# A macaron layer on one core: the second half's gathers moved behind the first half's returns, shared units split, all stages re-placed

## Chip, cores, metric

The kernel runs on one core of a Trainium2 chip. The metric is the device time of one execution in microseconds (us). TensorE is called PE, VectorE DVE, ScalarE ACT, GpSimd POOL and SyncE SP, as the profile does.

## What is computed

`x` has 4 batches of 512 tokens of width 128 (2048 tokens). The layer is a "macaron": half a feed-forward layer, attention, half a feed-forward layer, each on a layer-normalised input, each added to `x`:

```python
x = x + 0.5 * _L0_ffn_ref(_layernorm(x), ...)
x = x + _L0_attn_ref(_layernorm(x), ...)
x = x + 0.5 * _L0_ffn_ref(_layernorm(x), ...)

# _L0_ffn_ref, 8 experts, the best 2 of them per token, and one shared expert for all
probs = softmax(x_flat @ gate_w.T)
top_w, sel = jax.lax.top_k(probs, 2)
top_w = top_w / sum(top_w)
y = gelu(x_flat @ W1[e] + b1[e]) @ W2[e] + b2[e]      # weighted by top_w for the chosen e
out = sum(y * combine) + gelu(x_flat @ sW1 + sb1) @ sW2 + sb2
```

The attention has 8 query heads on 2 key heads and looks back 32 tokens within a batch, with a sink in the softmax.

## The kernel before

**Blocks and units.** Each of the two feed-forward layers is done in two halves of 1024 tokens (two batches). That gives four blocks, numbered 0 to 3: blocks 0 and 1 are the first layer, 2 and 3 the second. A block has 23 routed units (a tile of up to 128 tokens for one expert; here R0 to R3, name `("R", block, 0, RT)` in `ORDER`) and 8 shared units (4 for each of its two batches; S0 to S3). A unit has a first product (`first_product`, into the PSUM tile `z`), a gelu on ACT, and two steps later (`LAG`) a second product (`second_product`, into `y`).

**Steps.** `ORDER` numbers all 124 units; the number is the unit's step. Each engine runs a loop over the steps, and what else it does stands in a table: `PE_AT`, `ACT_AT`, `DVE_AT`, `POOL_AT` and `SP_AT` give each stage a step (behind the point its place in the step). Within a step the tables set the order of the instructions; the time comes from semaphores alone. Before: S0 has the steps 0 to 7, R0 8 to 30, R1 31 to 53, S1 54 to 61, R2 62 to 84, S2 85 to 92, R3 93 to 115, S3 116 to 123.

**The way of a routed block.** SP stores the normalised rows to `xr` (stage `rows`, `store_rows`). The router runs: PE turns the tokens (`tr`), makes logits, DVE picks the experts (`pick`, `gap`), PE counts positions (`pos`), DVE places them (`place`), PE tells the slots (`idx`), DVE makes the lists of experts (`tiles`, tile `te`) and of rows (`final`, `know_rows`). Then POOL fetches each unit's rows with an indirect DMA (`gather`, tile `xg`); PE turns two units' rows at a time (`xtr`, `turn_rows`), ACT evicts them (`xevict`, tile `xgt`), SP copies the expert's first weights into `w1_tile` (`copy_weights`; the profile writes `w_tile`). The result goes to `ysb` on ACT and back to DRAM by an indirect DMA of POOL (`give_back`, `yd`), one unit per step and three steps after its first product. When a block's last returns have landed, SP loads them (`load_y`, tile `yc`, which the profile calls `stage`), and DVE adds them to `x` (`comb`).

**What follows a block.** After block 0 DVE's combine gives `x` for the attention of batches 0 and 1 (`att_stats`, `att_pow` on POOL, `att_xn` on ACT, `att_tr` on PE, and on to `proj` and `xadd`), which runs among the units of R1; then block 2's router needs those. After block 1 the same goes for batches 2 and 3, among R2. Blocks 2 and 3 end in `comb` and a store.

**Lead of gathers and copies.** `ahead(r, by)` gives the step at which unit r's gather stands on POOL (8 routed units ahead) and its weight copy on SP (4 ahead), and no sooner than `KNOWN[block]`. A ring of 8 slots holds the rows (`xg`), one of 6 the weights.

Of the kernel before, what the change touches and what calls it, by code (L numbers as in the profile page):

```python
# [64 lines left out]
def routed_no(ph, i):  # L65
# [5 lines left out]
    ('pos', 0): 1.01, ('idx', 0): 6.51, ('xtr', 0, 0): 7.54, ('xtr', 0, 1): 8.51, ('xtr', 0, 2): 9.51,  # L71
    ('tr', 1, 0): 9.53, ('tr', 1, 1): 9.535, ('tr', 1, 2): 10.51, ('tr', 1, 3): 10.515, ('logits', 1): 11.51,
    ('turn_w',): 12.51, ('xtr', 0, 3): 13.51, ('xtr', 0, 4): 13.53, ('xtr', 0, 5): 13.54, ('pos', 1): 14.51,
    ('xtr', 0, 6): 18.01, ('idx', 1): 19.01, ('xtr', 0, 7): 20.01, ('xtr', 0, 8): 20.02, ('xtr', 0, 9): 25.51,
    ('xtr', 0, 10): 26.51, ('xtr', 0, 11): 28.51, ('xtr', 1, 0): 28.52, ('xtr', 1, 1): 32.51, ('xtr', 1, 2): 34.51,
# [1401 lines left out]
```

How the kernel before makes its waits and increments, by code:

```python
        def moved(eng, k):  # L340
            eng.wait_ge(m_done[k % MB], k // MB + 1)
# [5 lines left out]
        def result_out(eng, u):  # L348
            eng.wait_ge(y_used[Y_USE[u] % 2], Y_USE[u] // 2 + 1)
# [1 line left out]
        def landed(eng, r):  # L352
            eng.wait_ge(returned[r % YR], 16 * (r // YR + 1))
# [29 lines left out]
            def store_biases():  # L384
                sp.wait_ge(b_hi_done, 1)
                sp.dma_start(bd[0], b_hi[:, :]).then_inc(b_stored, 16)
                sp.wait_ge(b_split, 1)
                sp.dma_start(bd[1], b_lo[:, :]).then_inc(b_stored, 16)
# [1 line left out]
            def load_biases():  # L391
                sp.wait_ge(b_stored, 32)
                sp.dma_start(wb2[:, :, :], bd).then_inc(b_ready, 16)
# [16 lines left out]
            def store_rows(ph):  # L411
                for j in range(2):
                    sp.wait_ge(pre_lo_done, 2 * ph + j + 1)
                    rows = slice(j * TT * P, (j + 1) * TT * P)
                    sp.dma_start(xr[ph][rows].rearrange("(t p) r -> p t r", p=P), xs[ph % 2][:, TT * j:TT * (j + 1)])\
                        .then_inc(rows_stored[ph], 16)
# [1 line left out]
            def copy_weights(r):  # L418
                ph, _, i, _ = UNITS[ROUTED[r]]
                if i == 0:
                    sp.wait_ge(te_ready, ph + 1)
                if r == 0:
                    sp.wait_ge(w1_split, E)
                    sp.wait_ge(b1_ready, 1)
                if r >= WR:
                    sp.wait_ge(z_ready, ROUTED[r - WR] + 1)
                    sp.wait_ge(gelu_done, ROUTED[r - WR] + 1)
```

## Time and profile before

| | us |
|---|---|
| median of 3 runs (lowest, highest) | 375.26 (374.29, 377.11) |
| the profiled execution, its own time | 374.08 |
| span of the profiled execution, first to last instruction | 372.3 |
| PE busy in the span | 314.2 (84%) |
| ACT busy | 240.8 (65%) |
| POOL busy | 203.9 (55%) |
| DVE busy | 170.5 (46%) |

The median is 1.18 us above the profiled execution, and that one is 1.8 us longer than its span. A busy PE is not PE at its peak: ends of matmuls are modelled, and the engine also counts as busy at the half clock. All times in the rows below are from the span's start.

### The profile page before, as it was taken

To read this page: it belongs to the slowest core of one execution; us is meant where nothing else is said; L and a number is where in the kernel's file an instruction comes from. 1 tells how busy PE (TensorE), PEld (TensorE's weight loads), DVE (VectorE), ACT (ScalarE), POOL (GpSimd) and SP (SyncE) were. 2 spreads that over 40 slices of the span, in tenths; PEclk is the share of its full clock that TensorE was granted. 3 is DMA by queue.
4 is the path that set the end of the run, shared out by engine and by line. 5 is a ranking of instruction groups with operands and counts; after the bars stand their busy time and mean duration, and the time that the engine had idled before them with its cause. 6 is when DMAs were issued, how large, how long until landed. Compare 5 with 4: busy or idle time off the path is not lost.

```text
span 372.3 us, 10763 instructions
## 1 busy us (share of the span) xinstructions
PE 314.2 (84%) x3591; PEld 269.3 (72%) x3599; DVE 170.5 (46%) x623; ACT 240.8 (65%) x666; POOL 203.9 (55%) x220
## 2 busy tenths in 40 slices
PE   0692999999736998999895789999999699979991
PEld 0372988989636867899775588899888488868881
DVE  6997248400026479464782658826457330000005
ACT  4971577778624968959531787995974268847640
POOL 5206677777774875124417775745442577776500
PEclk9996799999976899999996999999999989989998
DMA  7793755555263244101136233324223745553131
GB/s 233 233 240 94 258 175 169 153 195 184 79 197 128 96 161 106 66 37 57 61 128 223 97 102 125 103 85 136 89 65 107 261 139 193 194 141 104 37 121 56
DMA packets 39222, 50.51 MB, mean 136 GB/s; under 512 B 5803, under 2 KB 23296, under 8 KB 39170
## 3 DMA queue, kind: packets, MB, share of 16 engines
...
## 4 chain that ended last, share of the span: by engine, by line
PE 52%; POOL 13%; issue 11%; DVE 11%; ACT 6%; DMA 6%; SPq 1%; DVEq 0%; ACTq 0%
PE y L619 16%; POOL xg L498 7%; PE z L583 5%; POOL yd L506 5%; PE y L634 4%; PE z L585 4%; PE z L584 4%; PE m L801 3%; PE y L622 3%; DVE x L1212 2%; DMA xg<-xr,from_row 2%; PE m L680 2%; PE m L654 2%; ACT h L877 2%; PE m L789 2%
## 5 line engine op out<-in xcount | busy, mean ns | idle before, releaser
L877 ACT ACTIVATE h<-z,w_tile 128x128 f32<-128x128 f32 x368 | 105.2, 373 | 40.0 <-PE z L585 37.6
L506 POOL DMA_INDIRECT yd<-ysb,to_row x92 | 91.7, 997 | 58.0 <-ACT ysb L890 38.6
L498 POOL DMA_INDIRECT xg<-xr,from_row x92 | 91.4, 993 | 58.6 <-issue 40.8
L619 PE MATMUL y<-w,h 128*128 x736 | 105.2, 288 | 0.0
L619 PEld LDWEIGHTS y<-w,h 128*128 128x128 f32 x736 | 93.0, 197 | 1.4
L583 PE MATMUL z<-xgt,w_tile 128*128 128x128 f16 x368 | 71.0, 229 | 12.1 <-ACT xgt L934 5.6
L584 PE MATMUL z<-xgt,w_tile 128*128 128x128 f16 x368 | 70.6, 227 | 0.0
L585 PE MATMUL z<-xgt,w_tile 128*128 128x128 f16 x368 | 70.6, 227 | 0.0
L583 PEld LDWEIGHTS z<-xgt,w_tile 128*128 128x128 f16 x368 | 37.2, 101 | 19.5 <-issue 8.6
L934 ACT ACTIVATE xgt<-m 128x512 f16<-128x512 f16 (+1 forms) x48 | 27.1, 590 | 25.0 <-PE m L680 24.8
L1112 DVE SCALAR_TENSOR_TENSOR x<-y,x 128x512 f32<-128x512 f32 x8 | 5.5, 690 | 79.7 <-PE y L639 79.7
L634 PEld LDWEIGHTS y<-w,h 128*128 128x128 f32 x256 | 35.9, 207 | 3.4
L1212 DVE SCALAR_TENSOR_TENSOR x<-stage,s_gate,x 128x128 f32<-128x128 f32 x64 | 19.1, 362 | 40.8 <-DMA stage<-yd 39.7
L585 PEld LDWEIGHTS z<-xgt,w_tile 128*128 128x128 f16 x368 | 37.6, 102 | 0.0
L584 PEld LDWEIGHTS z<-xgt,w_tile 128*128 128x128 f16 x368 | 37.4, 102 | 0.1
L634 PE MATMUL y<-w,h 128*128 128x128 f32 x256 | 36.9, 292 | 0.0
L882 ACT ACTIVATE h<-z,sb 128x512 f32<-128x512 f32 x32 | 21.9, 687 | 21.8 <-PE z L656 21.8
L680 PE MATMUL m<-ident,xg 128*128 128x128 f16 x184 | 19.2, 229 | 19.6 <-DMA xg<-xr,from_row 19.5
L890 ACT ACTIVATE ysb<-y 128x128 f32<-128x128 f32 x92 | 26.3, 286 | 12.6 <-PE y L622 11.6
L487 POOL TENSOR_TENSOR rstd<-ve,half 128x4 f32<-128x4 f32 x12 | 12.8, 1070 | 31.6 <-DVE ve L1081 31.5
L680 PEld LDWEIGHTS m<-ident,xg 128*128 128x128 f16 x184 | 11.9, 101 | 23.9 <-DMA xg<-xr,from_row 11.8
L914 ACT ACTIVATE xn<-x,nmr,rstd 128x128 f32<-128x128 f32 x48 | 19.7, 482 | 10.3 <-DVE nmr L1086 5.9
...
## 6 DMA issues: line engine op xcount, KB each, us to landing
...
xg<-xr,from_row POOLq DMA_INDIRECT x92, 2.7
yd<-ysb,to_row POOLq DMA_INDIRECT x92, 2.6
...
```

The source lines that it names most:

```text
L498: pool.indirect_dma_start(out=xg[:, r % XR, :], out_offset=None, in_=xr[ph], in_offset=bass.IndirectOffsetOnAxis(ap=from_row[:, ph, i:i + ...
L506: pool.indirect_dma_start(out=yd[ph], out_offset=bass.IndirectOffsetOnAxis(ap=to_row[:, ph, i:i + 1], axis=0), in_=ysb[:, r % YR, :], in_o ...
L583: pe.matmul(part, w[:, c, :], hi, start=(c == 0), stop=False, skip_group_check=True)
L584: pe.matmul(part, w[:, c, :], lo, start=False, stop=False, skip_group_check=True)
L585: op = pe.matmul(part, w[:, FC + c, :], hi, start=False, stop=True, skip_group_check=True)
L619: pe.matmul(to, h32[:, u % HB, c * P:(c + 1) * P], w2[:, bass.ds(e, 1), c, :].rearrange("p a d -> p (a d)"), start=(c == 0), stop=False, s ...
L634: op = pe.matmul(to[:, t * D:(t + 1) * D], h32[:, u % HB, t * P:(t + 1) * P], w2[:, SHARED, c, :], start=(c == 0 and t == 0), stop=False, ...
L680: op = pe.transpose(bank16(k)[:, at:at + P], xg[:, r % XR, part * D:(part + 1) * D], ident16[:, :])
L877: op = act.activation(h32[:, u % HB, cols], z[:, u % 2, cols], ACT.Gelu, bias=bias[:, c:c + 1], scale=1 / WS)
L890: act.activation(ysb[:, r % YR, :], y[:, Y_USE[u] % 2, 0:D], ACT.Copy).then_inc(y_used[Y_USE[u] % 2], 1)
L934: act.activation(xgt[:, (ph * PAIRS + q) % XT, 0:n].rearrange("p t k d -> p (t k d)"), bank16(k)[:, 0:2 * n * P], ACT.Copy)\
L1212: op = dve.scalar_tensor_tensor(to, yc[:, t, k, :], s_gate[:, ph, k, t:t + 1], to, ALU.mult, ALU.add)
```

## The change

It does four things. First, S1 and S3 are split: the first batch's four shared units stand ahead of the block's routed units, the other four behind them. After: S0 0 to 7, R0 8 to 30, first half of S1 31 to 34, R1 35 to 57, second half of S1 58 to 61, R2 62 to 84, S2 85 to 92, first half of S3 93 to 96, R3 97 to 119, second half of S3 120 to 123. Second, `KNOWN` is split in two lists, one for gathers and one for weight copies, and its second entry goes from 19 to 33, so that no row of block 1 is fetched before all of block 0's returns have been issued. Third, every stage gets a new place in all five tables. Fourth, SP's `rows` of block 1 goes from step 10 to 7. No computation is added or left out, and no tile changes its size.

```diff
-ORDER = [("S", 0, 0, 1), ("R", 0, 0, RT), ("R", 1, 0, RT), ("S", 1, 0, 1), ("R", 2, 0, RT), ("S", 2, 0, 1), 
-         ("R", 3, 0, RT), ("S", 3, 0, 1), ("none", 8)]
+ORDER = [("S", 0, 0, 1), ("R", 0, 0, RT), ("S", 1, 0), ("R", 1, 0, RT), ("S", 1, 1), ("R", 2, 0, RT), 
+         ("S", 2, 0, 1), ("S", 3, 0), ("R", 3, 0, RT), ("S", 3, 1), ("none", 8)]
...
-    ('gap', 3): 84.44, ('place', 3): 85.15, ('gates', 3): 89.37, ('tiles', 3): 89.45, ('final', 3): 90.14,
-    ('comb', 2, 0): 91.67, ('comb', 2, 1): 95.54, ('comb', 3, 0): 131, ('comb', 3, 1): 131.2,}
+    ('gates', 3): 90.73, ('tiles', 3): 90.85, ('comb', 2, 0): 91.62, ('final', 3): 92.98, ('comb', 2, 1): 95.67,
+    ('comb', 3, 0): 131, ('comb', 3, 1): 131.2,}
...
-    ('attention',): 0, ('rows', 1): 10, ('load_y', 0): 34, ('rows', 2): 52, ('load_y', 1): 57, ('rows', 3): 81,
-    ('load_y', 2): 88, ('store', 0): 95, ('store', 1): 99, ('load_y', 3): 119, ('store', 2): 131, ('store', 3): 131.5,}
+    ('attention',): 0, ('rows', 1): 7, ('load_y', 0): 34, ('rows', 2): 53, ('load_y', 1): 61, ('rows', 3): 83,
+    ('load_y', 2): 88, ('store', 0): 95, ('store', 1): 99, ('load_y', 3): 123, ('store', 2): 131, ('store', 3): 131.5,}
...
-KNOWN = [7, 19, 60, 90]
+ROWS_FROM, WEIGHTS_FROM = [7, 33, 61, 93], [7, 33, 61, 93]
...
-def ahead(r, by):
-
-    return max(STEP[ROUTED[max(r - by, 0)]], KNOWN[UNITS[ROUTED[r]].ph])
+def ahead(r, by, no_sooner):
+
+    return max(STEP[ROUTED[max(r - by, 0)]], no_sooner[UNITS[ROUTED[r]].ph])
...
-                    if ahead(r, WEIGHTS_AHEAD) == n:
+                    if ahead(r, WEIGHTS_AHEAD, WEIGHTS_FROM) == n:
                         copy_weights(r)
...
-                    if ahead(r, ROWS_AHEAD) == n:
+                    if ahead(r, ROWS_AHEAD, ROWS_FROM) == n:
                         gather(r)
```

Line numbers of the changed kernel are two higher than those of the kernel before.

**POOL, at the end of block 0.** `yd0` and `yd1` are the returns of blocks 0 and 1, `xr0` and `xr1` the stored rows that a gather reads. In the kernel before, from the last gather of block 0 on:

```order
L498 DMA xg<-xr0,from_row 128x256
L506 DMA yd0<-ysb,to_row 4992x128
L498 DMA xg<-xr1,from_row 128x256
L506 DMA yd0<-ysb,to_row 4992x128
L498 DMA xg<-xr1,from_row 128x256
```

and so on by turns for all 11 returns that are left, and then five turns with `yd1` before `L487 TENSOR_TENSOR rstd` (the powers of the attention's norm) is all through. In the changed kernel:

```order
L500 DMA xg<-xr0,from_row 128x256
L508 DMA yd0<-ysb,to_row 4992x128 x11
L500 DMA xg<-xr1,from_row 128x256 x11
L489 TENSOR_TENSOR rstd<-ve,half 128x4 x2
L508 DMA yd1<-ysb,to_row 4992x128
L500 DMA xg<-xr1,from_row 128x256
```

The 11 last returns of block 0 now stand in a row, then 11 gathers of block 1, then both powers, and only then the turns of returns and gathers of block 1.

**SP, ahead of the first routed unit.** `xr1<-xs1` is the store of block 1's rows, `w1_tile<-w1` the copy of a unit's weights, for which SP first loads the unit's expert from `te`. In the kernel before:

```order
L409 DMA sink<-in_L0_attn_sink_bias_dram 128x1
L429 TENSOR_LOAD te
L429 ISA x2
L430 ISA
L430 DMA w1_tile<-w1 128x516
```

and after six such copies `L415 DMA xr1<-xs1 128x4x256 x2`. In the changed kernel:

```order
L411 DMA sink<-in_L0_attn_sink_bias_dram 128x1
L417 DMA xr1<-xs1 128x4x256 x2
L431 TENSOR_LOAD te
L431 ISA x2
L432 ISA
L432 DMA w1_tile<-w1 128x516
```

The two stores have moved from behind the sixth copy to ahead of the first.

**DVE, at the same place.** `w<-stage,w` (`split_lo`) makes the low part of one expert's weights, `padded`, `from_row` and `to_row` are `final`, `xs<-xn,xs` the low part of block 1's rows that SP's stores wait for. In the kernel before:

```order
L1184 TENSOR_SCALAR te<-count 128x23 [waits router0]
L1232 SCALAR_TENSOR_TENSOR w<-stage,w 128x512 [waits w1_hi_done]
L1190 SCALAR_TENSOR_TENSOR padded<-m,pad 128x23 [waits m_ready]
L1192 CAST from_row<-m 128x23 [waits router0]
L1193 TENSOR_TENSOR to_row<-m,padded 128x23
L1232 SCALAR_TENSOR_TENSOR w<-stage,w 128x512 [waits m_done3,w1_hi_done]
L1232 SCALAR_TENSOR_TENSOR w<-stage,w 128x512 [waits w1_hi_done] x5
L1095 TENSOR_TENSOR xs<-xn,xs 128x4x128 [waits pre_hi_done] x2
```

In the changed kernel:

```order
L1186 TENSOR_SCALAR te<-count 128x23 [waits router0]
L1192 SCALAR_TENSOR_TENSOR padded<-m,pad 128x23 [waits m_ready]
L1194 CAST from_row<-m 128x23 [waits router0]
L1195 TENSOR_TENSOR to_row<-m,padded 128x23
L1234 SCALAR_TENSOR_TENSOR w<-stage,w 128x512 [waits m_done3,w1_hi_done]
L1234 SCALAR_TENSOR_TENSOR w<-stage,w 128x512 [waits w1_hi_done] x6
L1097 TENSOR_TENSOR xs<-xn,xs 128x4x128 [waits pre_hi_done] x2
```

Seven of the eight low parts stand behind `final` now, where six did.

## Rows read from the trace of the kernel before

**Rows 1.** PE's waits: what waited for what, us in total, times, longest.
```profile
PE m L680 <- DMA xg<-xr,from_row: 19.5, 11, 3.8
```
**Rows 2.** Chain that ended last, in order of time: start us, us, what.
```profile
105.77 4.00 DMA stage<-yd
...
119.17 0.63 PE m L735 x4
...
345.97 0.95 PE y L619 x8
347.85 0.95 PE y L619 x8
...
354.85 0.89 PE y L634 x8
356.39 0.89 PE y L634 x8
```
**Rows 3.** PE's timeline: start us, us, instruction, count, [idle before, what ended it].
```profile
20.30 1.05 PE L634 MATMUL y<-w,h 128*128 128x128 f32 x8
...
36.45 0.27 PE L583 MATMUL z<-xgt,w_tile 128*128 128x128 f16 x1 [1.69 <-DMA w_tile<-w]
...
37.68 2.02 PE L634 MATMUL y<-w,h 128*128 128x128 f32 x8
...
93.11 0.22 PE L622 MATMUL y<-wb,ones 2*128 x1
...
194.71 0.50 PE L634 MATMUL y<-w,h 128*128 128x128 f32 x3
...
199.87 0.29 PE L583 MATMUL z<-xgt,w_tile 128*128 128x128 f16 x1 [0.69 <-ACT xgt L934]
...
278.18 0.38 PE L654 MATMUL z<-xt,sw 128*128 128x512 f16 x1
```
**Rows 4.** SP's timeline of DMA issues: the first weight copies, block 1's rows, block 3's load.
```profile
33.52 6.75 SPq L430 DMA_DIRECT2D w_tile<-w  x6
40.31 1.22 SPq L415 DMA_DIRECT2D xr<-xs  x2
...
355.60 0.93 SPq L441 DMA_DIRECT2D stage<-yd  x2
```
**Rows 5.** DVE's timeline: low parts, block 3's lists and combine, the last combine.
```profile
28.84 3.70 DVE L1232 SCALAR_TENSOR_TENSOR w<-stage,w 128x512 f16<-128x512 f32 x6
32.46 1.34 DVE L1095 TENSOR_TENSOR xs<-xn,xs 128x512 f16<-128x512 f32 x2
...
289.60 0.17 DVE L1190 SCALAR_TENSOR_TENSOR padded<-m,pad 128x23 f32<-128x23 f32 x1
...
290.33 2.33 DVE L1212 SCALAR_TENSOR_TENSOR x<-stage,s_gate,x 128x128 f32<-128x128 f32 x8 [0.25 <-DVE to_row L1193]
...
365.06 4.53 DVE L1212 SCALAR_TENSOR_TENSOR x<-stage,s_gate,x 128x128 f32<-128x128 f32 x16
```
**Rows 6.** POOL's timeline: returns (yd), gathers (xg) and a power (rstd).
```profile
103.43 0.98 POOL L506 DMA_INDIRECT yd<-ysb,to_row  x1 [0.30 <-issue]
...
115.85 1.04 POOL L487 TENSOR_TENSOR rstd<-ve,half 128x4 f32<-128x4 f32 x1 [5.02 <-DVE ve L1081]
...
194.61 0.99 POOL L498 DMA_INDIRECT xg<-xr,from_row  x1 [8.10 <-issue]
...
290.90 1.00 POOL L498 DMA_INDIRECT xg<-xr,from_row  x1 [7.45 <-issue]
...
332.00 0.97 POOL L498 DMA_INDIRECT xg<-xr,from_row  x1 [0.30 <-issue]
...
353.20 0.97 POOL L506 DMA_INDIRECT yd<-ysb,to_row  x1 [0.84 <-ACT ysb L890]
```
**Rows 7.** DMA issues of the page: KB each, median us from issue to landing.
```profile
xg<-xr,from_row POOLq DMA_INDIRECT x92, 2.7
```
**Rows 8.** Span and mean granted clock of the core.
```profile
core 0: 372.3 us, clock 0.945
```

More of the change, by code:

```diff
@@ L70 @@
 PE_AT = {
[L71 to L75, printed above, removed]
@@ L89 @@
-    ('xtr', 2, 9): 79.51, ('tr', 3, 0): 79.52, ('tr', 3, 1): 79.525, ('xtr', 2, 10): 79.53, ('xtr', 2, 11): 79.54,
-    ('tr', 3, 2): 81.51, ('tr', 3, 3): 81.515, ('logits', 3): 82.51, ('pos', 3): 84.51, ('idx', 3): 89.51,
-    ('xtr', 3, 0): 92.51, ('xtr', 3, 1): 93.51, ('xtr', 3, 2): 96.51, ('xtr', 3, 3): 96.52, ('xtr', 3, 4): 96.53,
-    ('xtr', 3, 5): 101.01, ('xtr', 3, 6): 102.01, ('xtr', 3, 7): 104.51, ('xtr', 3, 8): 105.51, ('xtr', 3, 9): 107.01,
-    ('xtr', 3, 10): 110.51, ('xtr', 3, 11): 110.52,}
@@ new lines @@
+    ('pos', 0): 2.51, ('idx', 0): 7.01, ('xtr', 0, 0): 7.51, ('tr', 1, 0): 7.52, ('tr', 1, 1): 7.525,
+    ('tr', 1, 2): 7.53, ('tr', 1, 3): 7.535, ('xtr', 0, 1): 7.54, ('xtr', 0, 2): 9.51, ('xtr', 0, 3): 13.01,
+    ('xtr', 0, 4): 13.02, ('xtr', 0, 5): 13.03, ('logits', 1): 13.51, ('xtr', 0, 6): 15.01, ('xtr', 0, 7): 17.51,
+    ('xtr', 0, 8): 22.01, ('xtr', 0, 9): 23.51, ('pos', 1): 24.51, ('xtr', 0, 10): 25.01, ('xtr', 0, 11): 26.51,
+    ('idx', 1): 32.51, ('turn_w',): 32.52, ('xtr', 1, 0): 34.51, ('xtr', 1, 1): 36.51, ('xtr', 1, 2): 36.52,
@@ new lines @@
+    ('xtr', 1, 3): 37.51, ('xtr', 1, 4): 38.01, ('att_tr', 0): 39.51, ('att_tr', 1): 40.51, ('qk', 0): 40.52,
+    ('v', 0): 40.53, ('qk', 1): 41.01, ('scores', 0, 0): 43.01, ('scores', 0, 1): 43.02, ('xtr', 1, 5): 44.51,
+    ('v', 1): 44.52, ('xtr', 1, 6): 46.51, ('scores', 1, 0): 46.52, ('scores', 1, 1): 46.53, ('pt', 0, 0): 47.51,
+    ('pv', 0, 0): 48.51, ('pt', 0, 1): 48.52, ('xtr', 1, 7): 48.53, ('xtr', 1, 8): 48.54, ('pt', 1, 0): 48.55,
+    ('pv', 0, 1): 48.56, ('pt', 1, 1): 48.57, ('pv', 1, 0): 48.58, ('proj', 0): 48.59, ('pv', 1, 1): 48.6,
@@ new lines @@
+    ('xtr', 1, 9): 48.61, ('xtr', 1, 10): 48.62, ('proj', 1): 50.01, ('tr', 2, 0): 52.01, ('tr', 2, 1): 52.015,
+    ('xtr', 1, 11): 53.51, ('tr', 2, 2): 53.52, ('tr', 2, 3): 53.525, ('logits', 2): 55.01, ('pos', 2): 57.01,
+    ('idx', 2): 61.51, ('xtr', 2, 0): 61.52, ('xtr', 2, 1): 62.51, ('xtr', 2, 2): 64.51, ('att_tr', 2): 64.52,
+    ('qk', 2): 66.51, ('att_tr', 3): 67.51, ('xtr', 2, 3): 67.52, ('v', 2): 67.53, ('xtr', 2, 4): 67.54,
+    ('v', 3): 68.51, ('xtr', 2, 5): 68.52, ('qk', 3): 69.01, ('scores', 2, 0): 69.51, ('scores', 2, 1): 69.52,
@@ new lines @@
+    ('xtr', 2, 6): 70.51, ('xtr', 2, 7): 70.52, ('scores', 3, 0): 74.01, ('scores', 3, 1): 74.02, ('pt', 2, 0): 75.01,
[3 rows of a table added]
+    ('tr', 3, 3): 83.515, ('xtr', 2, 11): 83.53, ('logits', 3): 83.54, ('pos', 3): 85.51, ('idx', 3): 91.01,
+    ('xtr', 3, 0): 96.01, ('xtr', 3, 1): 97.51, ('xtr', 3, 2): 98.01, ('xtr', 3, 3): 99.51, ('xtr', 3, 4): 100.51,
+    ('xtr', 3, 5): 104.01, ('xtr', 3, 6): 106.01, ('xtr', 3, 7): 109.01, ('xtr', 3, 8): 110.01, ('xtr', 3, 9): 114.51,
+    ('xtr', 3, 10): 114.52, ('xtr', 3, 11): 116.01,}
@@ L138 @@
 POOL_AT = {
[L139 to L141 removed]
+    ('att_pow', 0): 38.11, ('att_pow', 1): 38.82, ('xres', 0): 41.17, ('xres', 1): 41.57, ('pow', 4): 49.48,
+    ('pow', 5): 51.87, ('att_pow', 2): 63.18, ('att_pow', 3): 66.37, ('xres', 2): 69.59, ('xres', 3): 69.78,
+    ('pow', 6): 79.04, ('pow', 7): 81.74,}
```

95 lines of the change are left out of this document (42 added, 53 removed), and 6 rows, old and new, of the table PE_AT.

## The prediction

> **What bounds the kernel now.** I read PE's waits first. The longest entry is PE waiting for gathered rows, 19.5 us in 11 waits [rows 1]. Then the chain that ended last: between a return of POOL at 103.43 and the load of block 0's results at 105.77 nothing but POOL's turns of returns and gathers leads it [rows 2, 6]. PE's timeline shows why. The last result of block 0 is finished at 93.11 + 0.22 = 93.33 [rows 3]; its return is issued at 103.43 [rows 6], ten microseconds later. A gather or a return costs POOL 1.284 us: from 290.90 to 332.00 stand 21 gathers and 11 returns, 41.10 / 32 [rows 6]. A turn of both is 2.57 us, while PE does a routed unit in 347.85 - 345.97 = 1.88 and a shared one in 356.39 - 354.85 = 1.54 [rows 2]. So where both stand on POOL, POOL sets the pace; elsewhere PE does. The attention of batches 0 and 1 hangs on the last return: combine, power at 115.85 [rows 6], PE's turn of the normalised tokens at 119.17 [rows 2].
>
> I follow five points: last return of block 0, first unit of R2 (before: 199.87), first unit of S2 (278.18) [rows 3], last return of block 3 (353.20) [rows 6], end (372.3).
>
> **Start: +3.2.** R0's first product waits for the first weight copy until 36.45 [rows 3]. That copy is issued at 33.52, right after the last low part, 28.84 + 3.70 = 32.54 [rows 4, 5]. Now one more low part (3.70 / 6 = 0.62) stands behind `final`, and I let `final` come 0.6 later, since PE tells the slots behind one more first product: low parts end at 33.8. Then SP must first store block 1's rows, which need the next two DVE instructions (1.34 [rows 5]): 35.1. The second store takes 1.22 / 2 = 0.61 [rows 4], the way to the first copy 33.52 - 32.54 = 0.98: 36.7, which is 3.2 late. Ends: 0, if the stage was covered by something I overlook, and 4.4, if the stores also hold the copy's data back by their 1.22. First product at 39.65.
>
> **R0 and its returns: -7.7.** From the first product to the last result it took 93.33 - 36.45 = 56.9. Three small pieces leave the block (slots of block 1, turned weights, one pair of turned rows); I take 1.5 for them, between 0 and one unit's 1.88. Result at 95.05, return 0.6 later (copy and issue, an allowance): 95.7 instead of 103.43. POOL keeps up: its 12 turns end as before, and the 10 returns behind gain 1.88 - 1.28 = 0.6 each on PE.
>
> **Head of R1.** The first gather of block 1 follows at 97.0. In R2 the first product came 199.87 - 194.61 = 5.26 after the first gather [rows 3, 6], so R1 starts at 102.3; PE has four shared units of S1 in front and waits for some 2 to 3 us. The combine can start 105.77 + 4.00 - 103.43 = 6.34 after the last return [rows 2, 6]: 102.0. But both powers now stand behind 11 gathers, three of which wait for turned rows: 97.0 + 11 x 1.26 = 110.9. DVE is no earlier, since the combine's second half waits behind the result of S1's first half, which PE makes in R1's second step. Power at 110.9 instead of 115.85. From there to PE's turn it was 119.17 - 115.85 = 3.32: 114.2; I take 114.5, as PE itself gets there at about 114. That is 4.7 early, of the 7.7. Ends: 7.7, if gathers and DVE wait for nothing, and 0, if they wait for each other. Block 1's first four weight copies now stand on SP just ahead of the load of block 0's results. They wait for slots that are free by then, and the shared units cover them: nothing; without the cover one costs 6.75 / 6 = 1.13 [rows 4].
>
> A rule of the Trainium skill speaks against such a row of gathers (page "SBUF — State Buffer", section "Who interferes with whom"): a DVE instruction with two SBUF inputs blocks a GpSimd instruction that reads SBUF. In the row, a gather issued beside the combine at 290.33 took 1.00 against 0.97 for one beside no such instruction [rows 5, 6]. By the row the burst loses nothing; by the rule it could lose up to the two combines beside it, 2 x 2.33 = 4.7, which is the time of the second rival.
>
> **To R2: -4.3.** After its turn at 119.17 PE worked until 194.71 + 0.50 = 195.21, 76.0 us [rows 2, 3]. What is left there now is 18 routed and 4 shared units in place of 15.7 and 8: 40.0 against 41.8, and one more pair of rows (0.2): -1.6. So PE is through at 114.5 + 74.4 = 188.9. But the slots of block 2 now come in the last step, so that no unit covers the way to R2: 0.1 + (290.90 - 289.60 = 1.3) from `final` to a gather [rows 5, 6], then 5.26: 6.7, where PE waited 199.87 - 195.21 = 4.7 before. R2 starts at 195.6. Ends for the 6.7: 5.3 (no list in the way) and 9.1 (an addition and a combine of 2.33 in it, as at R3).
>
> **R2: +1.0.** It took 278.18 - 199.87 = 78.3 [rows 3], and its work stays. The attention starts some 3 us later in it, and the router's logits stand right behind their turned tokens; I add 1.0, between 0 and one routed unit. S2 starts at 274.9, 3.3 early.
>
> **S2 to the last return: 0.0.** Before, the first gather came 290.90 - 278.18 = 12.7 after S2's first unit. Now lists of experts (1.3, as long as the way from `final` to the gather; an estimate) and a combine (2.33 + 0.25) stand ahead of `final` on DVE: 16.6. The first half of S3 covers this, so PE waits less at R3's head. But POOL's row is the same: 22nd gather 332.00 - 290.90 = 41.1 after the first, landing 2.7 or somewhat more [rows 7]: 44.3. Behind it PE has five routed units (9.4), one pair of rows, two steps with a shared unit (1.85 each) and the return (0.6): 14.1 in all. Last return 58.4 after the first gather, 62.3 before. 16.6 + 58.4 = 75.0, as before (353.20 - 278.18).
>
> **Tail: -5.5.** Before, 19.1 us followed the last return, as eight shared units stood behind. Now four do, and the way of the data is longer: load issued 355.60 - 353.20 = 2.4 later [rows 4, 6], 4.0 in flight [rows 2], combine 4.53, and 372.3 - 369.59 = 2.7 to the end [rows 5]: 13.6. PE's last products and the addition end about 1 us before the load lands. End for this term: -4, if the load takes longer.
>
> **Sum.** -3.3 + 0.0 - 5.5 = -8.8: a span of 363.5. The profiled execution was 1.78 longer than its span and 1.18 under the median: 366.5.
>
> **Rivals.**
>
> The start costs nothing (0.10): DVE's low parts end no later, or the copy isn't what R0 waits for. Against it speaks the wait of 1.69 for it [rows 3]. Then 363.3.
>
> The head of R1 eats the gain (0.22): 11 gathers, the powers behind them and the combine behind S1's result wait for each other, and the attention starts no earlier than before. For it: POOL, DVE and PE are each in order, and three gathers wait for PE. 366.5 + 4.7 = 371.2, at the edge of what can be told.
>
> The clock falls (0.11), the one that ends on the other side. The mean granted clock was 0.945 [rows 8], so (1 - 0.945) x 2 x 372.3 = 41 us at the lower of two levels, 1.2 GHz. There eight half products took 2.02 instead of 1.05 [rows 3]: 0.48 us are lost per us if PE sets the pace. R0's head was at this level after PE had waited, and now the heads of R0 and R2 wait longer and R1's anew. If the three together stay low 27 us longer, two thirds of what there was, it costs 13.0: 379.5. It decides from 26 us on; with less it only eats the gain. Against it: at the head of R3 the wait shrinks. The Trainium skill (page "TensorE: Matmul & The Clock Gate", section "HAM oscillation — how this bites in real kernels") has idle gaps bring the lower clock, at a loss of half the time spent there; the rows agree with 0.48.
>
> That the change doesn't do what it says is in the second rival: gathers behind returns are of use only if the attention starts earlier.
>
> **Chances.** Forecast 0.57, its own range 362 to 371. A measurement of this kernel can tell about 1% from no change, that is outside 371.5 to 379.0. Faster: 0.55 of the forecast, 0.10, and half of the second rival: 0.76. Same: the rest of these, 0.13. Slower: 0.11. The range for 8 in 10 reaches from 361.5 over the second rival to 374.5; the clock's case is left out.
>
> **What would show it.** Right: the first weight copy at about 36.7; POOL's last `yd` of block 0 near 95.7 and no gather of block 1 before; the first power near 111, ended by POOL's own queue; a wait of PE for gathered rows of some 6 us at R2's head; no wait at R3's head; block 3's load landing after PE's last product. Wrong: a power at 115 or later, R2's first unit at 200 or later, a clock under 0.90 at the heads' stretches taken together, or POOL's last returns behind PE by more than a unit.

## The result and the profile after

The changed kernel is a little faster: median 372.90 us (371.55 to 374.86, 12 runs), against 376.53 us (374.29 to 377.72, 12 runs) for the kernel before. The ratio is 0.9913, interval 0.9892 to 0.9933: 0.9%, where 2.3% were forecast. The direction was right, the size was not.

The profiled execution of the kernel before (374.08) lay 2.4 under the median of these 12 runs, that of the changed kernel (373.84) 0.9 over its own. So the spans (372.3 and 372.1) show almost none of the gain, and a difference of two us between the two traces is not a finding by itself. Some kernels had executions over 1.5% slower than their fastest (one of 6 in experiment 5, 3 of 12 in experiment 6, two of 6 in the first run of experiment 10, among them the one that was traced); they count in the medians, but not in the ratios.

The core's span and clock answer to [rows 8], PE's waits to [rows 1]:

```profile
core 0: 372.1 us, clock 0.943
```

```profile
PE m L682 <- DMA xg<-xr,from_row: 18.4, 11, 5.8
...
PE z L585 <- DMA w_tile<-w: 2.7, 1, 2.7
PE m L771 <- DVE v L1265: 2.4, 1, 2.4
```

The wait for gathered rows, which the edits were aimed at, went from 19.5 to 18.4. There are still 11 waits, and the longest grew from 3.8 to 5.8. Two waits are new or longer: the first weight copy, and one for `v`. The mean clock is nearly the same (0.945 before).

PE's timeline at the points followed, beside [rows 3]:

```profile
41.34 0.27 PE L585 MATMUL z<-xgt,w_tile 128*128 128x128 f16 x1 [2.72 <-DMA w_tile<-w]
...
100.78 0.27 PE L682 MATMUL m<-ident,xg 128*128 128x128 f16 x2 [0.70 <-DMA xg<-xr,from_row]
104.38 0.29 PE L682 MATMUL m<-ident,xg 128*128 128x128 f16 x2 [3.33 <-DMA xg<-xr,from_row]
105.36 0.29 PE L585 MATMUL z<-xgt,w_tile 128*128 128x128 f16 x1 [0.69 <-ACT xgt L936]
...
106.61 2.02 PE L636 MATMUL y<-w,h 128*128 128x128 f32 x8
...
119.64 0.30 PE L737 MATMUL m<-ident,xn 128*128 128x128 f32 x1 [0.52 <-ACT xn L916]
...
200.67 0.27 PE L585 MATMUL z<-xgt,w_tile 128*128 128x128 f16 x1 [0.81 <-ACT xgt L936]
...
281.29 0.61 PE L656 MATMUL z<-xt,sw 128*128 128x512 f16 x1
...
342.28 0.29 PE L682 MATMUL m<-ident,xg 128*128 128x128 f16 x2 [1.24 <-DMA xg<-xr,from_row]
...
343.86 2.02 PE L621 MATMUL y<-w,h 128*128 x8
```

Both second products of 2.02 stand behind a wait of PE and take twice what others take (1.05 in [rows 3]): they ran at the lower of the two clocks.

POOL's timeline, beside [rows 6]:

```profile
96.31 0.97 POOL L508 DMA_INDIRECT yd<-ysb,to_row  x1 [0.84 <-PE m L717]
97.66 0.98 POOL L500 DMA_INDIRECT xg<-xr,from_row  x1 [0.38 <-issue]
98.95 0.96 POOL L500 DMA_INDIRECT xg<-xr,from_row  x1 [0.30 <-issue]
...
102.70 0.97 POOL L500 DMA_INDIRECT xg<-xr,from_row  x1 [0.30 <-issue]
103.98 0.95 POOL L500 DMA_INDIRECT xg<-xr,from_row  x1 [0.30 <-issue]
...
112.55 0.94 POOL L500 DMA_INDIRECT xg<-xr,from_row  x1 [2.63 <-PE m L682]
116.39 1.04 POOL L489 TENSOR_TENSOR rstd<-ve,half 128x4 f32<-128x4 f32 x1 [2.89 <-DVE ve L1083]
...
222.19 2.50 POOL L514 TENSOR_TENSOR xres<-x,bo 128x512 f32<-128x512 f32 x2
...
297.53 1.00 POOL L500 DMA_INDIRECT xg<-xr,from_row  x1 [10.36 <-issue]
...
358.39 0.97 POOL L508 DMA_INDIRECT yd<-ysb,to_row  x1 [0.84 <-ACT ysb L892]
```

SP's DMA issues (beside [rows 4]) and DVE's timeline (beside [rows 5]):

```profile
34.95 0.97 SPq L417 DMA_DIRECT2D xr<-xs  x2
37.25 19.78 SPq L432 DMA_DIRECT2D w_tile<-w  x12
...
98.65 0.92 SPq L443 DMA_DIRECT2D stage<-yd  x2
```

```profile
29.98 4.30 DVE L1234 SCALAR_TENSOR_TENSOR w<-stage,w 128x512 f16<-128x512 f32 x7
...
102.51 2.32 DVE L1214 SCALAR_TENSOR_TENSOR x<-stage,s_gate,x 128x128 f32<-128x128 f32 x8 [4.40 <-DMA stage<-yd]
111.99 0.69 DVE L1114 SCALAR_TENSOR_TENSOR x<-y,x 128x512 f32<-128x512 f32 x1 [7.16 <-PE y L641]
112.59 2.31 DVE L1214 SCALAR_TENSOR_TENSOR x<-stage,s_gate,x 128x128 f32<-128x128 f32 x8
...
221.25 4.12 DVE L1254 TENSOR_SCALAR stage<-q_hi,head 128x512 f16<-128x512 f16 x4
```

The points side by side, us from the start of the span:

| point | before | forecast | after | after - before |
|---|---|---|---|---|
| R0's first product | 36.45 | 39.65 | 41.34 | +4.9 |
| last return of block 0 | 103.43 | 95.7 | 96.31 | -7.1 |
| first power of the attention | 115.85 | 110.9 | 116.39 | +0.5 |
| PE's turn of the normalised tokens | 119.17 | 114.5 | 119.64 | +0.5 |
| R2's first unit | 199.87 | 195.6 | 200.67 | +0.8 |
| S2's first unit | 278.18 | 274.9 | 281.29 | +3.1 |
| last return of block 3 | 353.20 | 349.9 | 358.39 | +5.2 |
| end | 372.3 | 363.5 | 372.1 | -0.2 |

The first term came true (-7.1 of -7.7 at the last return) and was gone twenty us later, at the attention's power. R2 and R3 then lost 4.4, and the tail gave 5.4 back. The experiments take these places one by one.

### The profile page after: what moved, and what is told of

Its sections match the earlier page's. It is cut to its first block, busy times and chain, and to the rows that moved or that the text cites. A ratio compares the mean times of both kernels' runs of the same rounds, so it can differ in the third digit from the quotient of the medians.

```text
span 372.1 us, 10771 instructions
## 1 busy us (share of the span) xinstructions
PE 315.5 (85%) x3599; PEld 268.9 (72%) x3599; DVE 173.6 (47%) x623; ACT 239.9 (64%) x666; POOL 202.2 (54%) x220
## 4 chain that ended last, share of the span: by engine, by line
PE 42%; POOL 16%; DVE 14%; issue 12%; DMA 9%; ACT 6%; SPq 1%; DVEq 0%; POOLq 0%; ACTq 0%
PE y L621 12%; POOL xg L500 9%; POOL yd L508 6%; DMA xg<-xr,from_row 5%; PE z L585 4%; PE m L803 3%; PE z L587 3%; PE z L586 3%; PE y L636 3%; DVE stage L1254 2%; PE y L624 2%; PE m L791 2%; ACT h L879 2%; DVE x L1214 2%; DMA x<-in_L_attn_x_dram 2%
## 5 line engine op out<-in xcount | busy, mean ns | idle before, releaser
L500 POOL DMA_INDIRECT xg<-xr,from_row x92 | 89.8, 976 | 60.4 <-issue 38.8
L621 PE MATMUL y<-w,h 128*128 x736 | 103.6, 285 | 0.0
L585 PE MATMUL z<-xgt,w_tile 128*128 128x128 f16 x368 | 70.1, 227 | 10.9 <-issue 4.3
L587 PE MATMUL z<-xgt,w_tile 128*128 128x128 f16 x368 | 69.8, 226 | 0.0
L586 PE MATMUL z<-xgt,w_tile 128*128 128x128 f16 x368 | 69.7, 226 | 0.0
L636 PE MATMUL y<-w,h 128*128 128x128 f32 x256 | 37.9, 298 | 0.0
L682 PE MATMUL m<-ident,xg 128*128 128x128 f16 x184 | 19.4, 226 | 18.5 <-DMA xg<-xr,from_row 18.4
L682 PEld LDWEIGHTS m<-ident,xg 128*128 128x128 f16 x184 | 11.7, 100 | 22.7 <-issue 12.7
L1214 DVE SCALAR_TENSOR_TENSOR x<-stage,s_gate,x 128x128 f32<-128x128 f32 x64 | 18.1, 347 | 8.4 <-DMA stage<-yd 8.0
```

The source lines that it names most:

```text
L500: pool.indirect_dma_start(out=xg[:, r % XR, :], out_offset=None, in_=xr[ph], in_offset=bass.IndirectOffsetOnAxis(ap=from_row[:, ph, i:i + ...
L585: pe.matmul(part, w[:, c, :], hi, start=(c == 0), stop=False, skip_group_check=True)
L586: pe.matmul(part, w[:, c, :], lo, start=False, stop=False, skip_group_check=True)
L587: op = pe.matmul(part, w[:, FC + c, :], hi, start=False, stop=True, skip_group_check=True)
L621: pe.matmul(to, h32[:, u % HB, c * P:(c + 1) * P], w2[:, bass.ds(e, 1), c, :].rearrange("p a d -> p (a d)"), start=(c == 0), stop=False, s ...
L636: op = pe.matmul(to[:, t * D:(t + 1) * D], h32[:, u % HB, t * P:(t + 1) * P], w2[:, SHARED, c, :], start=(c == 0 and t == 0), stop=False, ...
```

## The experiments

All start from the changed kernel unless something else is said. The diffs show table entries only. Each ratio is to runs of the kernel before on the same chip as the experiment, whose median there was between 376.1 and 377.4 us.

### 1. The stores of block 1's rows put back

```diff
-    ('rows', 1): 7
+    ('rows', 1): 10
```

> The changed kernel, with SP's store of block 1's rows put back from step 7 to step 10, behind the first weight copies. Theory (the stores hold up the first copy, and what R0 loses at its start goes through to the end): first copy issued near 34.6 instead of 37.25, first routed product near 38 instead of 41.34, last return of block 0 near 93.0 instead of 96.31, and the time 3 us under the changed kernel's, ratio to the kernel before 0.983. Rival (later waits swallow the start): last return of block 0 earlier by 3, R2's first unit where it was (200.7), ratio 0.991.

Measured: 371.48 us, ratio 0.9856 (0.9819 to 0.9893). SP's first weight copy and, in R3, POOL's first return of block 3:

```profile
35.36 6.56 SPq L432 DMA_DIRECT2D w_tile<-w  x6
```

```profile
311.12 1.01 POOL L508 DMA_INDIRECT yd<-ysb,to_row  x1 [2.75 <-ACT ysb L892]
```

The stores cost 37.25 - 35.36 = 1.9; the first product came at 39.56. R2 (198.28) and S2 (278.87) started 2.4 sooner, but the last return of block 3 only 0.5 sooner (357.86). POOL was ahead there: its first eleven gathers were through, and it waited 2.75 for the first result of R3, where the change waits 0.60. PE's wait for rows at R3's head (1.55) was followed by the lower clock, which held that first result back. So in this execution a gain at the start was waited away at R3's head. The gain came as far as S2, which is against the rival; the time lies between both.

### 2. The start put back as it was

```diff
-    ('xtr', 0, 1): 7.54, ('tr', 1, 0): 7.52 (to 7.535), ('rows', 1): 7
+    ('xtr', 0, 1): 8.51, ('tr', 1, 0): 9.52 (to 9.535), ('rows', 1): 10
```

(the evictions on ACT and DVE likewise)

> The changed kernel, with the start alone put back: rows of block 1 behind the first weight copies, turned tokens of block 1 and the second pair of turned rows behind R0's first product. Theory (behind the stores, which cost 1.9, the second pair of turned rows is what R0 waits for; the rest of the delay is DVE's low parts, 1.7 later): first product near 38.3 instead of 41.3 (39.6 with the stores alone put back), R2's first unit 3 us earlier than in the change, ratio 0.983 to 0.986. Rival (the stores alone): 39.5.

Measured: first product at 38.08, R2's first unit at 199.57 (1.1 sooner, not 3), 373.43 us, ratio 0.9896 (0.9857 to 0.9935). So what the change had moved ahead of R0's first product was the next wait behind the stores: 39.56 to 38.08. Two stages go back here at once, the second pair of turned rows (`xtr`) and block 1's turned tokens (`tr`). The trace of experiment 1 speaks for the pair: its second rows were turned at 38.46 and evicted until 39.49, and the product followed at 39.56. In the change itself this order cost nothing, since R0 waited 2.72 for the copy behind the stores. The end did not move, and again POOL waited 2.8 for R3's first result. The intervals of this run, of the one before and of the change overlap, so what the start is worth at the end, between nothing and 2 us, is left open.

### 3. The load of block 0's results behind R1's first unit

```diff
-    ('load_y', 0): 34
+    ('load_y', 0): 38
```

> The changed kernel, with the load of block 0's results (1 MB) behind the weight copy that waits for R1's first unit, so that block 1's first gathers have the DMA engines nearly to themselves. The attention is held up by it, so its time is not the question. Theory (the gathers land late because they share the DMA engines with the load): PE's wait for block 1's first rows near 1.5 instead of 4.04, R1's first unit near 102.5 instead of 105.4. Rival (the first gathers behind the returns are slow by themselves): wait near 4, first unit near 105.

Measured, in one execution: PE's timeline at R1's head.

```profile
101.91 0.28 PE L682 MATMUL m<-ident,xg 128*128 128x128 f16 x2 [0.94 <-DMA xg<-xr,from_row]
102.89 0.23 PE L585 MATMUL z<-xgt,w_tile 128*128 128x128 f16 x1 [0.69 <-ACT xgt L936]
```

PE's waits for the first rows are 0.19 + 0.94 = 1.13 instead of 0.70 + 3.33 = 4.03. R1 starts at 102.89, where 102.3 was forecast, and the products behind it ran at the full clock (granted 1.00 in 98 to 106, 0.91 in the change). But more than the load has moved: two weight copies of 258 KB, which stood right behind the load (issued from 100.70 on), now stand ahead of the gathers. So the load of 1 MB, issued at 98.65 between the first two gathers, and these two copies together made R1's head late: the DMA engines were busy 0.74 of 98 to 106 in the change and 0.17 here. What the load does without the copies wasn't tried. That transfers of SP and of POOL share the same DMA engines is also what the Trainium skill states (page "DMA: Bandwidth & Descriptors", section "Issuing engines are not separate DMA queues"); the run agrees, at 2.9 us.

### 4. Combine and powers ahead of the addition

```diff
-    ('comb', 0, 1): 36.36, ('att_stats', 0): 37.21, ('att_stats', 1): 37.93
+    ('comb', 0, 1): 35.3, ('att_stats', 0): 35.4, ('att_stats', 1): 35.5
-    ('att_pow', 0): 38.11, ('att_pow', 1): 38.82
+    ('att_pow', 0): 36.1, ('att_pow', 1): 37.1
```

> The changed kernel; on DVE the combine's second half and the attention's statistics of batches 0 and 1 stand ahead of the addition of S1's first result instead of behind it, and on POOL the two powers stand after nine and ten gathers of block 1 instead of eleven. PE keeps its order. Theory (three engines in order hold the attention, and PE's own place for the turn, behind five routed units, is the last of them): first power near 109 instead of 116.4, PE's turn still at 118.5 to 119.6, ratio to the kernel before 0.988 to 0.992. Rival (DVE's wait for the addition alone holds it): turn by 115, ratio 0.980.

Measured: 371.83 us, ratio 0.9845 (0.9819 to 0.9872). POOL's first power and PE's turn:

```profile
108.33 1.04 POOL L489 TENSOR_TENSOR rstd<-ve,half 128x4 f32<-128x4 f32 x1
```

```profile
118.56 0.41 PE L737 MATMUL m<-ident,xn 128*128 128x128 f32 x2
```

The power is 8 us sooner, the turn only 1.1: PE has its routed units first. Theory and numbers of the places agree. The time is 0.003 better than the theory's range; in R1 a wait of PE of 0.83 for DVE's maskings is gone as well.

### 5. Four gathers of block 1 among the last turns of block 0

```diff
-    ('pos', 1): 24.51, ('place', 1): 25.12, ('tiles', 1): 28.69, ('idx', 1): 32.51, ('final', 1): 32.9
+    ('pos', 1): 17.52, ('place', 1): 17.6, ('tiles', 1): 18.7, ('idx', 1): 22.51, ('final', 1): 22.9
+ROWS_AT = {23: 23, 24: 25, 25: 27, 26: 29}
...
-                    if ahead(r, ROWS_AHEAD, ROWS_FROM) == n:
+                    if ROWS_AT.get(r, ahead(r, ROWS_AHEAD, ROWS_FROM)) == n:
```

> The changed kernel, with block 1's slots told at step 22 and its first four gathers put singly among the last turns of block 0 (steps 23, 25, 27, 29), where POOL is idle 0.5 us of each step. Theory (R1's head is late because its first gathers land beside the load of block 0's results, PE then falls to the lower clock, and the whole chain product, addition, combine, power waits for that): last return of block 0 within 1 us of 96.3, R1's first unit near 101 instead of 105.4, no lower clock behind it, first power near 110 instead of 116.4, attention's first turn near 113 instead of 119.6, R2's first unit near 194.5 instead of 200.7, ratio to the kernel before 0.975. Rival (the row of gathers ahead of the powers holds the attention whatever PE does): power at 113 or later, turn at 118 or later, ratio 0.989.

Measured: 368.25 us, ratio 0.9776 (0.9742 to 0.981). R1's first unit stood at 101.92 without a wait for rows, but the last return came at 100.46, not at 96.3. POOL was not idle 0.5 us a step there, as I had said: its rows up to the last return follow one another every 1.28 us without a pause. Power at 113.21, turn at 117.29. So the last return is against the theory, the power in the rival's range, and the turn between both. Still the attention came 2.4 sooner, and the granted clock at R1's head was higher. The end of this execution came 5.5 sooner than the change's, and only 2.5 of it stood at R2's first unit (198.15): R2 was 1.1 shorter, and the rest came behind S2. What gave that no run shows. The same 14 us of the change and of this run (us, PE, PEld, DVE, ACT and POOL busy, then the clock):

```profile
98.00:112.00 14.00, 9.28 (x63) 8.08 (x63) 2.40 (x10) 3.93 (x11) 9.18 (x10) 0.76 0.56 179
```

```profile
98.00:112.00 14.00, 10.19 (x93) 8.91 (x92) 5.81 (x20) 7.09 (x20) 9.50 (x10) 0.91 0.61 203
```

### 6. The title edit undone

The tables of experiment 5, without `ROWS_AT`, and

```diff
-ROWS_FROM, WEIGHTS_FROM = [7, 33, 61, 93], [7, 33, 61, 93]
+ROWS_FROM, WEIGHTS_FROM = [7, 23, 61, 93], [7, 33, 61, 93]
```

> The changed kernel with its title edit undone: block 1's slots told at step 22 and its gathers again by turns with the returns of block 0 (from step 23 on, eight units ahead, as in the kernel before); the split of S1 and all else stay. Theory (the row of gathers behind the returns gains at the last return what it gives back at R1's head, so that by itself it is worth about nothing): last return of block 0 near 105 (96.3 in the change), R1's first unit near 101.5 with no wait, power near 118, turn near 121, ratio to the kernel before 0.988 to 0.997. Rival (the edit gains the 7 us that it takes off the last return, and other parts lose them): without it the time is 4 to 7 us over the changed kernel's, ratio 1.002 to 1.010.

Measured: 376.73 us, ratio 0.998 (0.9946 to 1.0015). The last return of block 0 comes at 104.91, the turn at 123.04:

```profile
119.79 1.04 POOL L489 TENSOR_TENSOR rstd<-ve,half 128x4 f32<-128x4 f32 x1 [10.11 <-DVE ve L1083]
```

Between theory and rival: gathers behind the returns gain 104.91 - 96.31 = 8.6 at the last return, 3.4 at the turn, and 0.998 - 0.9913, about 0.7% or 2.5 us, at the end.

### 7. S3's split alone, in the kernel before

```diff
-         ("R", 3, 0, RT), ("S", 3, 0, 1), ("none", 8)]
+         ("S", 3, 0), ("R", 3, 0, RT), ("S", 3, 1), ("none", 8)]
...
-    ('load_y', 3): 119
+    ('load_y', 3): 123
```

(and the turned rows of block 3 and their evictions four steps later)

> The kernel before, with nothing changed but S3: its first four units ahead of R3, its last four behind. Theory (what the change gains lies in the tail, since four shared units in place of eight stand behind the last return, and its other parts gave that back): from the last return to the end 13.6 us instead of 19.1, last return 58.4 to 60.9 after the first gather of block 3 instead of 62.3, ratio 0.975 to 0.983, better than the whole change. Rival (POOL's row, not PE's, sets the last return and the four units ahead of R3 only push it back): last return 2 to 6 us later, ratio 0.988 to 1.0.

Measured: 373.06 us, ratio 0.9911 (0.9877 to 0.9945), the same as the whole change. POOL's first gather and last return of block 3:

```profile
292.57 1.00 POOL L498 DMA_INDIRECT xg<-xr,from_row  x1 [7.45 <-issue]
...
355.56 0.97 POOL L506 DMA_INDIRECT yd<-ysb,to_row  x1 [0.83 <-ACT ysb L890]
```

The tail is 369.3 - 355.56 = 13.7, as forecast. But the last return comes 63.0 after the first gather, not 58.4 to 60.9: R3's first unit stands at 301.29 instead of 296.24, and POOL waits 1.4 for its result. The ratio falls into the rival's range. Four shared units moved from behind R3 to ahead of it take 5.4 off the tail and cost some of it at R3's head.

### 8. Block 3's rows known sooner

```diff
-    ('idx', 3): 91.01, ('gates', 3): 90.73, ('tiles', 3): 90.85, ('final', 3): 92.98
+    ('idx', 3): 90.01, ('gates', 3): 89.5, ('tiles', 3): 89.9, ('final', 3): 89.8
```

> The changed kernel, with block 3's list of rows (final) ahead of the combine of batch 0 and of an addition on DVE, and its slots told one step sooner on PE. Theory (from the first gather of block 3 to its last return POOL sets the pace, so each us by which the first gather comes sooner is a us at the end): first gather 11.8 after S2's first unit instead of 16.2, last return 72.7 after it instead of 77.1, time 4.4 us under the changed kernel's, ratio to the kernel before 0.980. Rival (PE sets the pace there): last return at most 1 us sooner, ratio 0.989 to 0.991.

Measured: 370.28 us, ratio 0.9839 (0.9808 to 0.987). The first gather stands 11.64 after S2's first unit (291.89 - 280.25), the last return 73.8 after it (354.08): 3.3 sooner than in the change, where 4.6 were gained at the first gather. The rest is again a wait of POOL for R3's first result:

```profile
308.67 1.01 POOL L508 DMA_INDIRECT yd<-ysb,to_row  x1 [2.93 <-ACT ysb L892]
```

### 9. POOL's residual additions, moved twice

```diff
-    ('xres', 2): 69.59, ('xres', 3): 69.78
+    ('xres', 2): 66.38, ('xres', 3): 66.39
```

> The changed kernel, with POOL's two residual additions of batches 2 and 3 (xres) moved from step 69 to step 66, right behind the second power, where DVE is idle. Theory (POOL's addition and DVE's masking of the queries hold each other up, 4.12 us in place of 1.14, and PE waits 2.43 for the values behind it): the masking takes 1.1 to 1.2, PE's wait of 2.43 is gone, R2 takes 78.3 instead of 80.6, time 2.3 to 4 us under the changed kernel's, ratio to the kernel before 0.982 to 0.985. Rival (the long masking has another cause): it stays near 4 us, ratio 0.991.

Measured: 372.78 us, ratio 0.9892 (0.9854 to 0.993). The masking takes 1.14 and PE's wait of 2.43 is gone, but another DVE instruction is now held. POOL and DVE:

```profile
215.70 2.48 POOL L514 TENSOR_TENSOR xres<-x,bo 128x512 f32<-128x512 f32 x2
```

```profile
215.75 2.46 DVE L1088 SCALAR_TENSOR_TENSOR nmr<-mv,rstd 128x4 f32<-128x4 f32 x1 [2.06 <-POOL rstd L489]
```

An instruction on 4 elements a partition, 0.16 elsewhere, takes 2.46 and ends 0.03 behind POOL's pair. PE's turn of the second batch comes at 220.08, 3.7 later, and the gain is gone. So the mechanism is shown, and the place was badly chosen. In the second try both stand a step later, where DVE has nothing to do:

```diff
-    ('xres', 2): 69.59, ('xres', 3): 69.78
+    ('xres', 2): 67.0, ('xres', 3): 67.01
```

> The changed kernel, with the two residual additions of batches 2 and 3 on POOL at step 67 (two steps earlier, and a step later than in the run where they came right behind the second power and met DVE's next instruction). Theory (POOL's addition of two SBUF operands and DVE's instructions exclude each other, and DVE has nothing to do for some 4 us there): no DVE instruction lengthened, PE's wait of 2.43 for the values gone, no wait over 1 for the second batch's normalised tokens, R2 takes 77.5 to 78.3 instead of 80.6, ratio to the kernel before 0.982 to 0.986. Rival (the time is not set there: PE or POOL take it back in R3): R2 shorter, but the ratio within 0.988 to 0.992.

Measured: 369.57 us, ratio 0.9795 (0.9766 to 0.9824). The same two DVE rows, and POOL's pair between them:

```profile
217.85 2.52 POOL L514 TENSOR_TENSOR xres<-x,bo 128x512 f32<-128x512 f32 x2
```

```profile
215.34 0.16 DVE L1088 SCALAR_TENSOR_TENSOR nmr<-mv,rstd 128x4 f32<-128x4 f32 x1 [2.07 <-POOL rstd L489]
...
223.11 1.14 DVE L1254 TENSOR_SCALAR stage<-q_hi,head 128x512 f16<-128x512 f16 x4
```

R2 takes 278.16 - 201.30 = 76.9 instead of 80.6; the theory had 77.5 at best, and 0.982. Two entries of one table are worth 1.2%, more than the whole change.

The additions of batches 0 and 1 hold DVE in the same way, and no experiment moved them. In the change:

```profile
126.46 2.49 POOL L514 TENSOR_TENSOR xres<-x,bo 128x512 f32<-128x512 f32 x2
```

```profile
126.79 2.73 DVE L1247 TENSOR_TENSOR q_lo<-q,q_hi 128x512 f16<-128x512 f32 x1 [0.77 <-ACT k_hi L964]
```

Other instructions of this form take 0.69.

### 10. The attention two steps earlier, and one step

Experiment 4, and every stage of the attention of batches 0 and 1 and of block 2's router 2.0 lower in the tables of PE, ACT, DVE and POOL, `ROWS_FROM[2]` and `WEIGHTS_FROM[2]` 59 instead of 61.

> The kernel of the experiment before (combine, statistics and powers freed), and all stages of the attention of batches 0 and 1 and of block 2's router two steps earlier on PE, ACT, DVE and POOL. Theory (then the way is free on all engines): powers near 109, PE's turn near 115 instead of 119.6, block 2's slots two units earlier, PE's wait for rows ahead of R2 under 3 instead of 6.0, R2's first unit near 196 instead of 200.7, ratio to the kernel before 0.979 to 0.982. Rival (R2's start hangs on PE's sum of work, not on the attention): first unit at 199 or later, ratio 0.988 to 0.991.

Measured: 394.09 us, ratio 1.0415 (1.0374 to 1.0457). Power 108.61 and turn 114.86 are as the theory said. Then it breaks:

```profile
169.49 1.04 POOL L489 TENSOR_TENSOR rstd<-ve,half 128x4 f32<-128x4 f32 x1 [17.29 <-DVE ve L1083]
```

A power two steps earlier on POOL stands ahead of returns and gathers of R1 and waits for DVE; how much of the loss this brings the run can't tell. And with 59, gathers of block 2 stand ahead of the last return of block 1, so the load behind that comes late, and PE waits 10.79 for the next normalised tokens. That second fault is mine and confounds the run. One step earlier, without that fault, on top of the four repairs of experiment 11:

> The kernel with the four repairs, and the attention of batches 0 and 1 and block 2's router one step earlier on PE, ACT, DVE and POOL. Theory (R2's head still waits some 6 for rows because the slots come behind the last shared unit): wait for rows ahead of R2 near 4.5, time 1 to 2 us under the kernel with the four repairs. Rival (as with two steps, the attention's products then outrun ACT and DVE, PE waits and falls to the lower clock): waits of PE for pt or probs in R1, time the same or up to 5 us over it.

Measured: 380.75 us, ratio 1.0114 (1.0092 to 1.0136), against 0.9648 without the step. POOL and PE:

```profile
167.22 1.04 POOL L488 TENSOR_TENSOR rstd<-ve,half 128x4 f32<-128x4 f32 x1 [10.54 <-DVE ve L1082]
```

```profile
140.20 0.29 PE L584 MATMUL z<-xgt,w_tile 128*128 128x128 f16 x1 [3.35 <-ACT xgt L935]
...
173.44 0.39 PE L681 MATMUL m<-ident,xg 128*128 128x128 f16 x2 [4.57 <-DMA xg<-xr,from_row]
```

The turn came at 114.90, 2.9 sooner, and R2's first unit at 210.06, 11.7 later. POOL's wait of 10.54 for the power is not what was lost: without the step POOL waits 10.85 at the same power (163.11). The trace shows two stoppages instead.

First, PE waits 3.35 for turned rows that ACT has still to evict. A step earlier, ACT's exponentials of the attention and their table loads (133.80 to 138.33) stand ahead of that eviction; without the step they stand behind it. PE then ran at the lower clock for a time (0.84 from 137 to 180, against 1.00 without the step). The attention's second scores came at 144.02, 2.6 later than without the step, where its turn had been 2.9 sooner. This is the rival's way, though the wait was for the eviction more than for `probs` (0.95 and 1.15), and the time, 17 us over, is more than the 5 it allowed.

Second, the power comes 4.1 later by then, and two gathers of block 1 stand behind it on POOL, where one did without the step: PE waits 4.57 for these rows. At the turn of block 2's tokens the kernel was 11.7 behind. How far the attention could be moved with ACT's exponentials left behind the eviction, and the powers behind the gathers, wasn't tried.

### 11. The repairs together

Experiments 2, 4, 8 and the second of 9 in one kernel.

> The changed kernel with four repairs at once: rows of block 1 behind the first weight copies and the turned tokens of block 1 and the second pair of turned rows behind R0's first product (the start as in the kernel before), final of block 3 ahead of the combine, combine and powers of block 0 ahead of the addition, residual additions of batches 2 and 3 at step 67. Theory (the losses lie in different places and add up: ratios so far 0.9856, 0.9839, 0.9845 and 0.9795 against 0.9913 for the change): ratio to the kernel before 0.955 to 0.962, 359 to 363 us. Rival (a saving in one place is waited away at the next, above all at R2's head and in POOL's row of R3): ratio 0.968 or more.

Measured: 363.63 us (362.34 to 365.39), ratio 0.9648 (0.9623 to 0.9673). First product 38.61, power 107.52, turn 117.83, R2 198.41, S2 274.50. Each repair's ratio over the change's 0.9913, multiplied with one another and with 0.9913, gives 0.964: the repairs add up. The theory's range (0.955 to 0.962) was missed all the same. It was too low because I took the start's 0.9856 of experiment 1 and not the 0.9896 of experiment 2. One wait that the repairs leave, or bring, is POOL's for R3's first result:

```profile
302.92 1.00 POOL L508 DMA_INDIRECT yd<-ysb,to_row  x1 [2.94 <-ACT ysb L892]
```

With four, and with two, of block 1's gathers among the last turns of block 0 (`ROWS_AT` of experiment 5; `{23: 29, 24: 31}`):

> The kernel with the four repairs, and block 1's slots told at step 22 with its first four gathers singly among the last turns of block 0. Theory (a mixture beats both ends: R1's head has its rows, and the last return is only 3 to 4 us later): last return near 99, R1's first unit near 100.5, no lower clock there, power near 111.5, turn near 113.5 instead of 117.8, ratio to the kernel before 0.951 to 0.957. Rival (the later return eats it): turn at 116 or later, ratio 0.963 to 0.967.

> The same with only the first two gathers among the last turns (steps 29 and 31). Theory (two rows are all that R1's first pair needs, at a price of 1 to 2.5 us at the last return): last return near 97, R1's first unit near 100.5, power near 109.5, turn near 112.5, ratio to the kernel before 0.948 to 0.955, under the one with four. Rival (the next pair lands beside the load and PE waits there instead): a wait of 2 or more ahead of R1's third unit, turn at 115 or later, ratio 0.957 to 0.965.

Measured with four: 365.25 us, ratio 0.9712 (0.9671 to 0.9752). Last return 97.20, R1's first unit 98.66, but the third and the fifth pair of rows keep PE waiting (2.49 and 2.62), and the turn is at 118.33: the rival, with a time over even its range. With two: 362.41 us (360.17 to 365.11), ratio 0.9642 (0.9591 to 0.9694). Last return 96.22, R1's first unit 100.03, smaller waits than the rival had (0.94 and 1.41), but turn (115.66) and time are the rival's. It can't be told from the kernel without early gathers. Both are some 3.5% under the kernel before and 2.7% under the change.

## Why the prediction was off

**Start, +3.2.** Measured +4.9. The stores cost 1.9 (experiment 1), the low parts ended 34.28 instead of 32.54, which is 1.7 late where I had 1.3, and the copy needed 41.3 - 37.25 = 4.1 behind the stores where it had needed 2.9 [rows 3, 4]. The whole lies above the upper end of 4.4 that I had named. Missed: the second pair of turned rows, moved ahead of R0's first product. It cost nothing here, behind the wait for the copy, but takes 1.5 of the gain when the stores go back (experiment 2, together with block 1's turned tokens).

**R0 and its returns, -7.7.** 96.31 for 95.7, which is in part luck: R0 started 1.7 later than forecast, and 1.1 of that was made up because R0 took 54.3 from its first product to its last result where I had 55.4.

**Head of R1, -4.7 at the turn.** This step failed, in the way of the second rival. I had the power wait for POOL's row of eleven gathers, to 110.9. It waited for DVE until 116.39, and DVE for PE's result of S1's first half until 111.99; the second half of the combine stands behind that addition. I had named that wait and taken PE to be there in time. Two costs had made PE late: the gathers landed beside the load of the same block's results and two weight copies (4.03 of waiting; 1.13 without them, experiment 3), so that R1's first unit came at 105.36 and not at 102.3; and the lower clock behind that wait doubled the next products. POOL's eleventh gather waited 2.63 for PE as well. Experiment 4 shows the price of the order on DVE, 8 us at the power; and that PE's own place for the turn holds nearly all of it back, which is a third queue that I had timed at 114 and that stood at 119.

**To R2.** Right in the sum but for its start, where two misses cancel: from the turn PE worked 193.08 - 119.64 = 73.4 (forecast 74.4), then 7.6 to R2's first unit (forecast 6.7).

**R2, +1.0.** Measured +2.3, and nearly 4 us were to be had. One trace alone would not tell 1.3 from nothing: the kernel of experiment 7, unchanged up to S2, took 79.7 for its R2 where the kernel before took 78.3. Six traces with the change's R2 took 79.7 to 80.9, and the cause is shown by the second try of experiment 9. I had counted the attention's later start and passed over a moved stage: POOL's residual additions, which now fell on DVE's masking (experiment 9). I had weighed the Trainium skill's rule on DVE and GpSimd (page "SBUF — State Buffer", section "Who interferes with whom") against gathers, where it costs nothing here, and not against POOL's residual additions, which read two SBUF operands of 512 elements a partition. There it holds: that section has whichever of the two starts first keep the shared port for the whole instruction while the other is fully blocked. The rows show 2.46 for 0.16, through two additions and not only one.

**S2 to the last return, 0.0.** Measured +2.1. The first gather stood 16.24 behind S2's first unit (forecast 16.6), POOL's row took 41.18 to its 22nd gather (forecast 41.1). Mis-sized is what follows: 19.7 where I had 3.2 + 14.1 = 17.3, because PE waited 1.24 for rows and then ran at the lower clock. I had priced no clock behind that wait. Of seven other traces with this S2 and R3 five show the same 77 us in all and two 79, so this is no chance of one trace.

**Tail, -5.5.** Right: 13.7 after the last return, -5.4. Experiment 7 shows the same tail by itself.

**Clock rival.** It did not come: 0.943 against 0.945. The lower clock moved from place to place with the waits.

**Where the forecast's 363.5 and the traced 372.1 part.** Of the 8.6 us between them, 5.2 arose at R1's head (+0.5 for -4.7), 1.3 in R2 and 2.1 behind S2; the tail was right. The two traces show 0.2 of the gain and the medians 3.6, so some 3 us stay that the traces can't place.

**Why the sum came to 0.9%.** S3's split alone gives 0.9911, the whole change 0.9913. The title edit is worth 0.7% (experiment 6), and by subtraction the new places of other stages took about as much away; with intervals of 0.2 to 0.4% on each ratio this is an estimate, and not tried. The additions of experiment 9 stand 1.2% from a free place. (In the kernel before they met a combine, which took 3.27 instead of 2.33; what they cost there wasn't tried.) The split of S1 wasn't tried alone.
